# A half-height matmul in the down projection is filled up to 128 rows with zeros

## The reference

```
gu = einsum('ech,ehf->ecf', xe, gate_up_proj)     # 256 tokens x 512 -> 2 x 192
g, u = split(gu, 2)
h  = silu(g) * u                                  # 256 tokens x 192
ye = einsum('eci,eih->ech', h, down_proj)         # 192 -> 512
```

## Time and profile before

| what | value |
|---|---|
| time, median of 3 runs | 2414.44 us (2411.25 to 2418.63) |
| profiled execution: span from first to last instruction | 2450.7 us |
| mean granted TensorE clock in it | 0.934 of full speed |
| PE busy, share of the span | 2104.8 us, 86% |
| DVE (VectorE) busy | 1749.9 us, 71% |
| ACT (ScalarE) busy | 1371.8 us, 56% |
| POOL (GpSimd) busy | 1125.8 us, 46% |
| matmuls of L1300, x128 | 63.8 us, mean 498 ns |
| matmuls of L1299, x128 | 51.1 us, mean 399 ns |
| first and last start of L1300 | 1722.2 and 2246.2 us |

### The profile page before, as it was taken

How to read it: one execution, slowest core, us unless ns; L and a number is a source line. 1 busy time by engine, 2 the same in 40 slices (tenths; PEclk the granted TensorE clock), 3 DMA queues, 4 the chain that set the end, 5 groups by cost and what they waited for, 6 DMA issues and landing times. The chain is left out here.

```text
span 2450.7 us, 43821 instructions
## 1 busy us (share of the span) xinstructions
PE 2104.8 (86%) x13313; PEld 1802.7 (74%) x13313; DVE 1749.9 (71%) x3146; ACT 1371.8 (56%) x2755; POOL 1125.8 (46%) x1093
## 2 busy tenths in 40 slices
PE   8999969999999999999999989982999999996000
PEld 6777758988899888988899877772888888884000
DVE  5899967876787677776787645553777777774657
ACT  3899946665676567665676532222566666663000
POOL 1455523332333223332333226664666666664675
PEclk9999979999999999999999999995999999997555
DMA  7444462012411051104300065432788888884775
GB/s 241 176 193 193 188 250 88 27 57 86 135 62 57 24 190 70 57 22 162 121 35 23 23 237 174 174 128 97 255 263 278 263 265 273 265 268 160 216 235 182
DMA packets 145296, 380.61 MB, mean 155 GB/s; under 512 B 19584, under 2 KB 37120, under 8 KB 140544
## 3 DMA queue, kind: packets, MB, share of 16 engines
q1 hardware_dynamic: 120576, 311.61, 37.1%
q0 software_dynamic: 24576, 67.20, 8.3%
HBM read 252.78 MB, written 125.96 MB: 155 GB/s over the span
## 5 line engine op out<-in xcount | busy, mean ns | idle before, releaser
L603 PE MATMUL p_S<-p_kT,p_q 128*128 128x512 f32 (+3 forms) x1920 | 475.0, 377 | 31.8 <-DMA p_q<-qk_scratch 25.1
L603 PEld LDWEIGHTS p_S<-p_kT,p_q 128*128 128x128 f32 x1920 | 324.7, 190 | 81.0 <-issue 27.3
L795 POOL TENSOR_SCALAR p_prob<-p_prob,p_inv,p_part 128x1024 f32<-128x1024 f32 x128 | 153.0, 1196 | 496.1 <-DVE p_inv L748 496.1
L615 PE MATMUL p_TP<-p_ident,p_prob 128*128 128x128 f32 x2176 | 303.5, 274 | 1.8 <-DVE p_pT1l L754 1.8
L795 POOL TENSOR_SCALAR p_prob<-p_prob,p_inv 128x128 f32<-128x128 f32 (+7 forms) x256 | 191.5, 748 | 241.4 <-DVE p_inv L743 241.4
L732 DVE TENSOR_REDUCE p_nmax<-p_S 128x1 f32<-128x1024 f32 (+7 forms) x256 | 251.7, 983 | 23.1 <-PE p_S L603 22.1
L615 PEld LDWEIGHTS p_TP<-p_ident,p_prob 128*128 128x128 f32 x2176 | 245.5, 141 | 25.9 <-DVE p_pT1l L754 5.6
L690 ACT CAST p_pT1h<-p_TP 128x512 fp32r<-128x512 f32 (+3 forms) x320 | 154.8, 526 | 153.5 <-PE p_TP L615 153.3
L690 ACT CAST p_pT0h<-p_TP 128x512 fp32r<-128x512 f32 (+3 forms) x320 | 155.1, 527 | 150.4 <-PE p_TP L615 149.2
L634 PE MATMUL p_O<-p_pT0h,p_v 128*128 128x256 f32 x1088 | 227.6, 293 | 6.0 <-DVE p_pT0l L754 6.0
L634 PE MATMUL p_O<-p_pT1h,p_v 128*128 128x256 f32 x1088 | 226.0, 292 | 5.6 <-issue 3.2
(11 more groups left out here) (212 smaller groups left out, 5061.0 us busy)
## 6 DMA issues: line engine op xcount, KB each, us to landing
p_w_raw<-in_gu SPq DMA_DIRECT2D x64, 768.0 KB
qk_scratch<-p_qout SPq DMA_DIRECT2D x80, 512.0 KB, 2.6
o_scratch<-p_oT SPq DMA_DIRECT2D x128, 256.0 KB, 2.1
p_ot<-o_scratch SPq DMA_DIRECT2D x32, 1024.0 KB
y_scratch<-p_y SPq DMA_DIRECT2D x128, 256.0 KB
p_q<-qk_scratch SPq DMA_DIRECT2D x15, 2048.0 KB, 9.2
p_w_raw<-in_gu SPq DMA_DIRECT2D x64, 256.0 KB
v_scratch<-p_vout SPq DMA_DIRECT2D x16, 512.0 KB, 3.2
```

The costliest lines, as they stand in the source:

```text
L603: mm = nc.tensor.matmul(out, x, y, start=(n == 0), stop=(n == 2))
L615: mm = nc.tensor.transpose(TP[n % 2][:, s % 4, :], prob[u % KEEP][:, s * P:(s + 1) * P], ident[:])
L795: nc.gpsimd.tensor_scalar(prob[k][:, cols], prob[k][:, cols], inv[:, k:k + 1], scale, ALU.mult, ALU.mult).then_inc(normed, 1)
```

## The change

The matmul of L1300 takes all 128 partitions of the high h buffer and of `t_x[k]`. For the product to be the same, the 64 partitions of h that do not belong to the expert must be zero. So there are two h buffers, one for even and one for odd experts, both cleared at the start; each expert writes only its own half of the left-over columns. A semaphore `h_blank` makes GpSimd wait for both clearings once.

```diff
-        h = sb("h", [P, 2, CAP])
+        h = [sb(f"h{k}", [P, 2, CAP]) for k in range(2)]
...
-                half, _ = rest(k)
...
-                    mm = nc.tensor.matmul(py[c][:], h_s[HI][half, 1, cols], t_x[k][half, :], start=False, stop=True)
+                    mm = nc.tensor.matmul(py[c][:], h_s[HI][:, 1, cols], t_x[k][:], start=False, stop=True)
...
-                nc.scalar.copy(h_s[LO][other, 1, :], h[half, 1, :]).then_inc(h_cross, 1)
+                nc.scalar.copy(h_s[LO][other, 1, :], h[k][half, 1, :]).then_inc(h_cross, 1)
...
-                nc.vector.tensor_tensor(h[half, 1, :], prest[half, :], sgt[half, :], ALU.mult).then_inc(h_rest, 1)
+                nc.vector.tensor_tensor(h[k][half, 1, :], prest[half, :], sgt[half, :], ALU.mult).then_inc(h_rest, 1)
...
-            nc.vector.memset(h[:], 0.0)
+            for k in range(2):
+                nc.vector.memset(h[k][:], 0.0).then_inc(h_blank, 1)
...
-                nc.gpsimd.tensor_scalar(h_s[HI][:], h[:], 1.0, 1.0, ALU.mult, ALU.mult).then_inc(h_part, 1)
+                nc.gpsimd.tensor_scalar(h_s[HI][:], h[k][:], 1.0, 1.0, ALU.mult, ALU.mult).then_inc(h_part, 1)
...
+            pool.wait_ge(h_blank, 2)
             pool.wait_ge(table_ready, 3)
```

More of the change, by code:

```diff
@@ L1176, in stage_experts @@
         h_part, h_split, h_cross = sem("h_part"), sem("h_split"), sem("h_cross")
-        downed, y_a, y_b = sem("downed"), sem("y_a"), sem("y_b")
+        downed, y_a, y_b, h_blank = sem("downed"), sem("y_a"), sem("y_b"), sem("h_blank")
         y_out = [[sem(f"y_out{k}{c}") for c in range(CH)] for k in range(2)]
@@ L1421, in gate @@
                     dve.wait_ge(h_cross, e)
-                nc.vector.tensor_tensor(h[:, 0, :], pgu[:, 1, :], sg[:], ALU.mult).then_inc(h_main, 1)
+                nc.vector.tensor_tensor(h[k][:, 0, :], pgu[:, 1, :], sg[:], ALU.mult).then_inc(h_main, 1)
                 dve.wait_ge(rest_silued, e + 1)
-                nc.vector.tensor_tensor(h[half, 1, :], prest[half, :], sgt[half, :], ALU.mult).then_inc(h_rest, 1)
+                nc.vector.tensor_tensor(h[k][half, 1, :], prest[half, :], sgt[half, :], ALU.mult).then_inc(h_rest, 1)
             def rows(i, k):
@@ L1475, in split_h @@
                 wait_alone(pool, passed, h_rest, e + 1)
-                nc.gpsimd.tensor_scalar(h_s[HI][:], h[:], 1.0, 1.0, ALU.mult, ALU.mult).then_inc(h_part, 1)
+                nc.gpsimd.tensor_scalar(h_s[HI][:], h[k][:], 1.0, 1.0, ALU.mult, ALU.mult).then_inc(h_part, 1)
                 wait_alone(pool, passed, h_part, e + 1)
-                nc.gpsimd.tensor_tensor(h_s[LO][:], h[:], h_s[HI][:].bitcast(F32), ALU.subtract).then_inc(h_split, 1)
+                nc.gpsimd.tensor_tensor(h_s[LO][:], h[k][:], h_s[HI][:].bitcast(F32), ALU.subtract).then_inc(h_split, 1)
             def step(i, k):
```

## The result

| | us |
|---|---|
| before, median of 4 runs | 2414.62 (2411.25 to 2418.63) |
| after, median of 4 runs | 2391.80 (2387.59 to 2396.58) |
| ratio after / before | 0.9911, 95% interval 0.9895 to 0.9926 |
| forecast | 2389, range 2364 to 2402 |

What follows compares the result with a forecast made beforehand. Bound by a loop of VectorE's queue, `t_lo`, even down and gate_up (16.61 us per pair), not TensorE alone. 31 x 0.77 = 23.9 plus 1.3 gives 25.2 us off 2414.4: 2389.2 us, range 2364 to 2402.

Steps and rivals of the forecast that it cites:

- The price of a 64-row matmul: Around L1300: switching between 128 and 64 rows leaves gaps; 128 rows save 0.77 us per expert, bounds 0 and 0.8.
- Which part counts: Expert stage: only one down and one gate_up per pair lie in the limiting loop, so 0.77 us per pair counts.
- The wait of 0.18 us for `t_lo`: Before the even down: it starts 0.18 us late, hidden in PE's busy time, so VectorE's queue sets the 16.61 us pair.
- VectorE's 8.37 us: VectorE's queue from the odd expert's L1422 to the end of L1405: taken to stay 8.37 us.
- The bounds: For VectorE's 8.37 us: 7.39 if L1405 never waits, 9.0 if L1477's own 0.6 us comes on top.
- The rival that made it slower by the other order: VectorE and GpSimd, odd step: L1477 ahead of L1393 stretches 8.37 us up to 9.4; 2420 us, chance 5%.
- the forecast's sum for that order: VectorE's queue with L1477 ahead of L1393: 3.6 + 1.6 + 1.2 + 0.6 + 1.4 = 8.4 us.
- The sum: Whole run: 31 intervals at 0.77 give 23.9 us, the last two downs 1.3, together 25.2 us saved.
- gathers, "6 us stay for 4.5": Between a gather's issue and its transposes: 6 us remain to cover the median 4.5 us to landing, so no cost.
- The cover of `cross`, "0.7 us left": From `split_h` to `cross`: 4.29 us hides behind gate_up and turn, which fall from 5.14 to 5.03; no cost.
- 36 us of the profiled execution: Profiled execution exceeds the timed median by 36 us, place unknown; the 25.2 us saving is taken off the median unchanged.

Runs made afterwards that it cites:

- odd experts alone: Kernel before with two h buffers, only the odd experts' last matmul on 128 rows, the even ones still on 64: 2414.37 us, ratio 1.0005 to before.
- the split loads: Changed kernel with the making of `t_x` split over both steps and the `t_raw` load split, each half issued a step earlier: 2381.53 us, ratio 0.9869 to before.
- even experts only: Kernel before with two h buffers, only the even experts' last matmul on 128 rows, the odd ones still on 64: 2395.43 us, ratio 0.9931 to before.
- the split making alone: Half of VectorE's `t_x` work moved to the even step: in the kernel before 2411.37 us (0.9995), in the changed kernel 2376.63 us (0.9857).
- The last experiment: The fastest version with its last matmul back on 64 rows of the same buffers: 2446.56 us against 2450.68 for before, ratio 0.9984.
- the fastest version: Changed kernel with `t_x` making and `t_raw` load split, and the high part of h made by ScalarE: 2365.68 us, ratio 0.9792 to before.

## Why the prediction was right, and where it was not

- **The price of a 64-row matmul.** Forecast 0.66 per down and 0.11 on gate_up; measured 0.67 and 0.10. That it is the change of height was shown by putting the two together: 0.38 us less per pair with both still 64 rows.
- **Which part counts.** The wait of 0.18 us for `t_lo`, read from two distances of 0.97 and 0.79 us in a PE that looked full, was the step that halved the forecast. With `t_x` made in two steps both distances were 0.79 us; odd experts alone gave nothing (1.0005), and the even distance grew from 0.97 to 1.71; and the pair came to 15.84 us as computed.
- **VectorE's 8.37 us.** It stayed 8.37, with L1390 first by 0.05 us, as taken. The bounds were real on one side: without GpSimd's low part the two operations took 1.39 us and the pair came to TensorE's floor. The rival that made it slower by the other order didn't come up here; with the other order (the split loads) L1393 took 0.48 us and L1398 0.50 us longer, so the forecast's sum for that order, in which only the first of the two waits, was too short; that kernel was still faster than the changed one, because its `t_x` work is split.
- **The sum.** In the traces, from the first even down to the end of the last odd one: 525.8 us before (1721.12 to 2246.95), 502.4 after (1693.72 to 2196.09), 23.5 saved against 25.2 forecast. The parts were off more than the sum. The 31 intervals gave 20.0, not 23.9: the late gather took 4.2 back (19.10 + 16.81 - 2 x 15.85), the first interval 0.3, and the last gave 0.6 more. The last two downs gave 3.5, not 1.3: before, the last ten matmuls mostly ran 0.43 us apart, at a granted clock of 0.50, after 0.23 apart, at 1.00, with PE idle for 2.77 us ahead of them in both:

```profile
2241.40:2246.90 5.50, 5.47 (x10) 2.90 (x10) 0.00 (x0) 0.00 (x0) 0.00 (x0) 0.50 0.02 8
2193.40:2196.00 2.60, 2.52 (x10) 1.80 (x10) 0.00 (x0) 0.03 (x1) 0.00 (x0) 1.00 0.06 24
```

The mechanism was right. That these errors nearly cancel, so that the total is off by only 1.7 us in the traces, is luck.
- **The step that failed: gathers, "6 us stay for 4.5".** The cover was computed against the median. One gather per run is issued 1.8 us late, the same one in all 14 traces (a pause of 2.10 to 2.17 us). In five of them (the changed kernel, even experts only, both with the split making alone, and the split loads) its issue started 0.22 to 0.79 us behind VectorE's subtraction and took 1.80 to 2.37 us, the data landed 7.2 to 7.8 us after its start, and two intervals were 4 to 6 us too long together. In the other nine it started 0.16 to 1.12 us ahead of the subtraction, or 0.03 behind it, took about 0.96 us, landed after 3.3 to 4.9, and no interval is long there. In the changed kernel 1.8 us of lateness and 3.3 over the median of 4.5, less the 1.5 us of cover, make the 3.6 that PE waited. The matmuls behind that wait ran at a granted clock of 0.51 for some 3 us, which adds to the loss. In this kernel the shorter pair had moved the issue and the subtraction past each other. No experiment set out to test this.
- **The cover of `cross`, "0.7 us left".** I measured it against the down projection. The next in ScalarE's queue is SiLU, and it had 0.47 us of idle time before and none after (1954.05 + 0.40 against 1954.43). It didn't cost here; with the even experts alone it cost 0.2 us in every second pair.
- **36 us of the profiled execution.** The forecast said that nothing in the profile says where they lie, and took the 25.2 us off the median all the same. The traces put 20.4 us ahead of the first even down, 12.7 behind the last odd one and none between, so the step was sound. The last experiment shows the same: 1718.6 us ahead and 200.9 behind, against 1698.1 and 190.4 in the fastest version. What causes it isn't shown. It need not be another chip: the record gives one chip number to the runs of before at 2450.68 us and to others at 2412.66.

## What to carry to other kernels

A matmul on half of the rows between full ones is not cheaper; here it cost 0.4 us for each excursion, so fill it with zeros or put all such matmuls side by side. Before multiplying a saving by its count, look for the loop that sets the period: compare start-to-start distances of the steps that should be alike, since a short wait can hide in a busy share of 100%. The time that covers a step must be held against the next instruction in the queue and against the slowest case, not against the consumer and the median.

## What the runs showed of the hardware

- Going from 128 rows to 64 and back: 0.10 us in, 0.19 out, 0.10 on the matmul after, at 2.4 GHz, with the loader idle 0.36 to 0.37 us ahead and 0.24 to 0.37 behind. Two 64-row matmuls in a row pay it once.
- VectorE's subtraction with two inputs in SBUF and GpSimd's elementwise operations took turns, whole instructions long. Started 0.01 us ahead, GpSimd's operation took 0.63 us and VectorE's 2.24; started 0.05 us behind, GpSimd's took 2.19 and VectorE's 1.76.
- One indirect gather behind 2.10 to 2.17 us of idle time of GpSimd, in the 27th of 32 pairs, in all 14 kernels. The cause of the pause was not looked for. What follows it depended on 0.2 us: ahead of VectorE's subtraction, or 0.03 us behind it, the issue took 0.96 us and the data landed after 3.3 to 4.9; 0.22 us and more behind it, up to 2.37 and up to 7.8.
- Behind 2.77 us without a matmul the granted clock was 0.50 in the kernel before and 1.00 in the changed one, at the same place of the program.
